# Half-empty weight block of an FFN filled with the low parts, and three reorderings, in a one-core transformer kernel

## The reference

```
base_up, base_gate = xt @ w_up.T, xt @ w_gate.T            # 704 hidden features
for e in range(8):                                          # LoRA experts, rank 16
    c = sum(where(sf == e, wf, 0))                          # weight of expert e, top 2 of 8
    h_e = silu(base_up + lo_up[e]) * (base_gate + lo_gate[e])
    ch = c * h_e
    mixed_h += ch
    lora_down += 2 * (ch @ down_A[e].T @ down_B[e].T)
out = mixed_h @ w_down.T + lora_down
```

## Time and profile before

| | |
|---|---|
| median of 3 runs | 557.07 us (556.97 to 557.43) |
| profiled execution | 557.08 us, its span 555.3 us |
| PE (matmul) | 523.4 us busy, 94% of the span |
| DVE / ACT / POOL | 402.6 (73%) / 310.6 (56%) / 126.9 (23%) |
| mean granted TensorE clock | 0.996 of full speed |
| DMA | 14.25 MB, mean 26 GB/s |

### The profile page before, as it was taken

The page is one execution under the profiler, slowest core; times in us unless marked ns, Lnnn a source line. Parts: engine busy times, 40 slices in busy tenths (PEclk is TensorE's granted clock), DMA queues, the critical chain, the costliest instruction groups (busy, mean ns, idle before and its releaser), DMA issues. The chain is left out here.

```text
span 555.3 us, 9124 instructions
## 1 busy us (share of the span) xinstructions
PE 523.4 (94%) x3049; PEld 441.6 (80%) x3049; DVE 402.6 (73%) x897; ACT 310.6 (56%) x768; POOL 126.9 (23%) x272
## 2 busy tenths in 40 slices
PE   5998899999999979999989999999998999999996
PEld 4777799999998967688878888757777778878885
DVE  5534465665665878799787899866886677878767
ACT  3655877688687643474343455988662254333332
POOL 2332434344243310000000003569433000000000
PEclk9999999999999999999999999999999999999999
DMA  7320000000002103000030000000000000000101
GB/s 267 112 78 1 18 22 2 1 1 2 2 2 102 47 1 138 1 1 1 5 129 0 2 0 1 1 1 2 1 0 2 0 1 1 1 1 0 39 1 38
DMA packets 5790, 14.25 MB, mean 26 GB/s; under 512 B 624, under 2 KB 2928, under 8 KB 5744
## 3 DMA queue, kind: packets, MB, share of 16 engines
q1 hardware_dynamic: 5744, 13.66, 6.9%
HBM read 12.61 MB, written 1.05 MB: 25 GB/s over the span
## 5 line engine op out<-in xcount | busy, mean ns | idle before, releaser
L167 PE MATMUL psum<-xT_hl,ffn_w_hl 128*128 128x512 f32 x312 | 77.8, 397 | 3.1 <-DVE f_t L1232 3.1
L167 PE MATMUL psum<-f_um,ffn_w_hl 128*128 128x512 f32 x288 | 72.6, 399 | 1.4 <-DVE f_t L1232 1.3
L167 PEld LDWEIGHTS psum<-xT_hl,ffn_w_hl 128*128 128x128 f32 x312 | 56.3, 188 | 15.0 <-issue 4.0
L167 PEld LDWEIGHTS psum<-f_um,ffn_w_hl 128*128 128x128 f32 x288 | 53.2, 188 | 14.8 <-DVE f_um L1244 3.1
L1129 ACT ACTIVATE f_sil<-psum 128x512 f32<-128x512 f32 (+1 forms) x48 | 28.6, 596 | 63.1 <-PE psum L167 62.8
L1232 DVE TENSOR_TENSOR f_t<-psum,f_sil 128x512 f32<-128x512 f32 (+1 forms) x48 | 33.2, 691 | 30.0 <-ACT f_sil L1129 29.3
L691 DVE TENSOR_TENSOR pT_hl<-psum,pT_hl 126x360 fp32r<-126x360 f32 (+1 forms) x44 | 23.6, 537 | 42.9 <-ACT pT_hl L598 42.9
L167 PE MATMUL psum<-wo_hl,oT_hl 128*128 128x256 f32 x384 | 50.8, 282 | 4.0 <-DVE oT_hl L697 4.0
L167 PE MATMUL psum<-xT_hl,wq_hl 128*128 128x512 f32 x192 | 52.3, 407 | 1.9 <-ACT qT L566 1.9
L167 PEld LDWEIGHTS psum<-wo_hl,oT_hl 128*128 128x128 f32 x384 | 47.7, 188 | 7.5 <-DVE oT_hl L697 5.9
L566 ACT ACTIVATE qT<-psum 128x512 f32<-128x512 f32 x32 | 34.9, 1091 | 31.6 <-PE psum L167 31.6
(11 more groups left out here) (238 smaller groups left out, 1130.4 us busy)
## 6 DMA issues: line engine op xcount, KB each, us to landing
w_raw<-in_wq SPq DMA_DIRECT2D x4, 512.0 KB, 4.1
w_raw<-in_wo SPq DMA_DIRECT2D x4, 512.0 KB, 3.2
ffn_w_raw<-in_ffn SPq DMA_DIRECT2D x3, 576.0 KB, 5.7
...
```

The lines of the kernel that those rows point to most:

```text
L167: i = e.matmul(dst, lhs(a), rhs(b), start=start and n == 0, stop=stop and n == len(TERMS) - 1, **kw)
```

## The change

**FFN block 5.** The down weights of block 5 are stored twice, in rows 0 to 63 and in 64 to 127 (`twice`); once, in the first FFN at ACT step 4, ACT copies the low parts of rows 0 to 63 over the high parts of these rows (`s_fwx`). The first 64 partitions of `tt` are set to zero by POOL (4 memsets a FFN), so ch and mix are zero there. ACT copies rows 64 to 127 of ch (two slots) and of mix to rows 0 to 63 of the low part, DVE writes the low part of rows 64 to 127 as before. The products of block 5 in `down` are then two matmuls with the same weight tile instead of three.

**Block 6.** `base_lora(6)` stands ahead of `second(5)` on PE. On DVE `masked` part 3 of half 1 moves ahead of `gated(4, 1)`, and parts 4 to 7 ahead of `gated(6, 0)`.

**Attention.** `oT_lo` stands ahead of `add` in each DVE step, `norm0` directly behind it, ahead of `add`; `exps` of units 0, 1, 2 lie behind the v copy of their step, unit 0 in two parts, and `recip` of units 0 and 1 one step later; query projection 7 goes to bank 7 and doesn't wait for the evacuation of projection 6.

Besides, several one-time semaphores of the router are merged in two (`top_dve`, `top_pe`); the instructions and their order are the same, and these lines are left out here.

```diff
@@ -315,7 +315,9 @@

 LAG_T, LAG_P, LAG_O, LAG_F, LAG_Y = 2, 3, 4, 5, 6
 FIRST_UNITS = {NJ - 6: 0, NJ - 4: 1, NJ - 2: 2}
-RECIPS = {NJ - 5: 0, NJ - 3: 1}
+RECIPS = {NJ - 4: 0, NJ - 2: 1}
+EXPS = {NJ - 6: (0, (0, 1)), NJ - 5: (0, (2, 3)), NJ - 4: (1, range(NB_Q)), NJ - 2: (2, range(NB_Q))}
+Q_PAIR = 2 * GROUP - 1
 NF = len(FIRST_UNITS)
 q_chunk = {NF - 1 + i: [GROUP + i] for i in range(3)}
...
@@ -439,10 +441,10 @@
         g, h = n // (2 * GROUP), n % GROUP
         half = n // GROUP % 2
         e.wait_ge(s_wl, WQ[g])
-        if n:
+        if n and n != Q_PAIR:
             e.wait_ge(s_qt, n)
         for k in range(KB):
-            m = three(e, bank(6), lambda w: wq_hl[:, g % 2, w, k, h * HD:(h + 1) * HD],
+            m = three(e, bank(7 if n == Q_PAIR else 6), lambda w: wq_hl[:, g % 2, w, k, h * HD:(h + 1) * HD],
                       lambda w: xT[:, w, k, HALF * half:HALF * half + HALF], k == 0, k == KB - 1)
         m.then_inc(s_q, 1)
...
         e.wait_ge(s_wl, WO[g])
+        e.wait_ge(s_qt, Q_PAIR + 1)
         if n:
             e.wait_ge(s_add, n)
...
-        e.activation(qT[:, HALF * half:HALF * half + HALF, h], bank(6), ACT.Copy,
+        e.activation(qT[:, HALF * half:HALF * half + HALF, h], bank(7 if n == Q_PAIR else 6), ACT.Copy,
...
-    def exps(u):
...
-        for n in range(parts):
+        for n in range(parts) if some is None else some:
             m = e.activation(p[:, n, :], p[:, n, :], ACT.Exp, bias=NEGM[0:rows, u % 4, n:n + 1],
                              accum_out=DEN[0:rows, u % 4, n:n + 1])
-        m.then_inc(s_exp, 1)
+        if n == parts - 1:
+            m.then_inc(s_exp, 1)

...
     for j in range(NJ):
-        if j in FIRST_UNITS:
-            exps(FIRST_UNITS[j])
         e.wait_ge(s_v, j + 1)
         e.activation(v_hl[0:NK[j], HI, j, :], bank(4 + j % 2)[0:NK[j], :], ACT.Copy).then_inc(s_vhi, 1)
         if j < GROUP:
             q_evac(j)
+        if j in EXPS:
+            exps(*EXPS[j])
     e.wait_ge(s_par, 16)
     e.wait_ge(s_cf, 16)
     e.activation(gw_hl[:, GW_PARTS:], cf[:, 0:GW_PAD - GW_PARTS], ACT.Copy, scale=0.0)
@@ -710,14 +714,15 @@
             recip(i - 1)
         if 0 <= i - LAG_P < NU:
             pT_lo(i - LAG_P)
+        if 0 <= i - LAG_F < NU:
+            oT_lo(i - LAG_F)
+        if i == NU + 1:
+            early(phase, "norm0", e)
         if i in y_tile:
             add(y_tile[i])
             if y_tile[i] >= (KV - 1) * NT:
                 early(phase, "stats", e, y_tile[i] % NT)
-        if 0 <= i - LAG_F < NU:
-            oT_lo(i - LAG_F)
-        for step, stage in ((NU, "veps0"), (NU + 1, "norm0"), (NU + 2, "lo0"), (NU + 3, "logits_copy0"),
-                            (NU + 4, "split0")):
+        for step, stage in ((NU, "veps0"), (NU + 2, "lo0"), (NU + 3, "logits_copy0"), (NU + 4, "split0")):
             if i == step:
                 early(phase, stage, e)

...
             da=4, dd0=4, dd=4, dh=4, dl=4, y=4, add=4)
+F_EVENTS |= dict(z=4, cx=4, mx=2)
...
@@ -1036,14 +1044,29 @@
             need(e, "dd0", 2)
         for s in range(SLOTS):
             need(e, "chl", 2 * i + s + 1)
-            m = three(e, bank(6 + s), lambda w: blk(w, b, FB_DA, ER),
-                      lambda w: ch_hl[:, i % 2, s, w, :], b == 0, b == HB - 1)
             if b == HB - 1:
+                if s == 0:
+                    e.wait_ge(s_fwx, 1)
+                need(e, "cx", 2 * h + s + 1)
+                for w in (HI, LO):
+                    m = e.matmul(bank(6 + s), blk(HI, b, FB_DA, ER), ch_hl[:, i % 2, s, w, :],
+                                 start=False, stop=w == LO)
                 m.then_inc(FS["da"], 1)
+                continue
+            three(e, bank(6 + s), lambda w: blk(w, b, FB_DA, ER),
+                  lambda w: ch_hl[:, i % 2, s, w, :], b == 0, False)
         if h == 1 and b == 0:
             need(e, "add", 2)
         need(e, "mxl", i + 1)
+        if b == HB - 1:
+            need(e, "mx", h + 1)
         for t in range(HT):
+            if b == HB - 1:
+                for w in (HI, LO):
+                    m = e.matmul(bank(4 + t // 2)[:, (t % 2) * D:(t % 2 + 1) * D],
+                                 mix_hl[:, i % 2, w, t * P:(t + 1) * P], blk(HI, b, FB_DN, D),
+                                 start=False, stop=False, skip_group_check=True)
+                continue
             m = three(e, bank(4 + t // 2)[:, (t % 2) * D:(t % 2 + 1) * D],
                       lambda w: mix_hl[:, i % 2, w, t * P:(t + 1) * P],
                       lambda w: blk(w, b, FB_DN, D),
@@ -1068,12 +1091,10 @@
                 weigh(1)
             if i == MASK_STEP + 1:
                 masks(e, 1, 0)
-            if i == MASK_STEP + 2:
-                second(i - 1)
             base_lora(e, i)
         if i == N:
             early(phase, "tr0", e)
-        if 2 <= i <= N and i != MASK_STEP + 2:
+        if 2 <= i <= N:
             second(i - 1)
         if i == MASK_STEP + 1:
             masks(e, 1, 1)
...
@@ -1145,6 +1166,9 @@
             need(e, "d", i - 1)
         need(e, f"ch{s}", i + 1)
         e.activation(ch_hl[:, i % 2, s, HI, :], ch[:, i % 2, s, :], ACT.Copy).then_inc(FS["chh"], 1)
+        if i % HB == HB - 1:
+            e.activation(ch_hl[0:REST, i % 2, s, LO, :], ch[REST:P, i % 2, s, :],
+                         ACT.Copy).then_inc(FS["cx"], 1)

     def hi_parts(i):
         if first and i == 0:
@@ -1156,6 +1180,9 @@
             weights_out(1)
         need(e, "mix", i + 1)
         e.activation(mix_hl[:, i % 2, HI, :], mix[:, i % 2, :], ACT.Copy).then_inc(FS["mxh"], 1)
+        if i % HB == HB - 1:
+            e.activation(mix_hl[0:REST, i % 2, LO, :], mix[REST:P, i % 2, :],
+                         ACT.Copy).then_inc(FS["mx"], 1)

     def lora_hi(h):
         for n, cols in enumerate(LORA_COLS):
@@ -1185,6 +1212,11 @@
             split(5)
         if i == 2:
             split(6, 7)
+        if i == MASK_STEP and first:
+            e.wait_ge(s_fwl, HB + 1)
+            stacked = slice(F_BLK + (HB - 1) * FB + FB_DN, F_BLK + HB * FB)
+            e.activation(w_hl[0:REST, HI, stacked], f32(w_hl[0:REST, LO, stacked]),
+                         ACT.Copy).then_inc(s_fwx, 1)
         if i == N - 5:
             early(phase, "w_hi0", e)
...
@@ -1285,6 +1317,8 @@
             need(e, "wbc", 2 * h + 2)
         if i >= 2:
             need(e, "chl", 2 * (i - 1))
+        if i % HB == HB - 1:
+            need(e, "z", 2 * h + s + 1)
         e.tensor_tensor(ch[:, i % 2, s, :], tt[:, s, :], wb[:, s, half(h)], ALU.mult).then_inc(FS[f"ch{s}"], 1)

...
@@ -1296,16 +1330,18 @@

     def lo_slot(i, s):
         need(e, "chh", 2 * i + s + 1)
-        e.tensor_tensor(ch_hl[:, i % 2, s, LO, :], ch[:, i % 2, s, :], f32(ch_hl[:, i % 2, s, HI, :]),
-                        ALU.subtract).then_inc(FS["chl"], 1)
+        rows = slice(REST, P) if i % HB == HB - 1 else slice(0, P)
+        e.tensor_tensor(ch_hl[rows, i % 2, s, LO, :], ch[rows, i % 2, s, :],
+                        f32(ch_hl[rows, i % 2, s, HI, :]), ALU.subtract).then_inc(FS["chl"], 1)

     def lo_parts(i):
         if i < N - 1:
             lo_slot(i, 0)
         lo_slot(i, 1)
         need(e, "mxh", i + 1)
-        e.tensor_tensor(mix_hl[:, i % 2, LO, :], mix[:, i % 2, :], f32(mix_hl[:, i % 2, HI, :]),
-                        ALU.subtract).then_inc(FS["mxl"], 1)
+        rows = slice(REST, P) if i % HB == HB - 1 else slice(0, P)
+        e.tensor_tensor(mix_hl[rows, i % 2, LO, :], mix[rows, i % 2, :],
+                        f32(mix_hl[rows, i % 2, HI, :]), ALU.subtract).then_inc(FS["mxl"], 1)

     def lora_mask(h):
         if h:
@@ -1338,12 +1374,12 @@
             a_lo(1)
         if i == MASK_STEP + 1:
             masked(1, 0, 1)
+        if i == MASK_STEP + 2:
+            masked(1, 4, 5, 6, 7)
         if i < N and i != 1:
             slot(i, 0)
         if i == MASK_STEP + 1:
-            masked(1, 2)
-        if i == MASK_STEP + 2:
-            masked(1, 4, 5)
+            masked(1, 2, 3)
         if i == HB + 3:
             early(phase, "stats", e, *range(HT))
             early(phase, "veps0", e)
@@ -1363,10 +1399,7 @@
                 slot(1, 0)
             lo_parts(i - 1)
         if i == MASK_STEP + 1:
-            masked(1, 3)
             mask_diff(1)
-        if i == MASK_STEP + 2:
-            masked(1, 6, 7)
         if 1 <= i <= 4:
             split(i + 3)
         if i == MASK_STEP - 2:
@@ -1386,7 +1419,12 @@

 def pool(e):
     ln["rstd"](e, 1)
-    early(phase, "rstd0", e)
+    for h in range(2):
+        for s in range(SLOTS):
+            need(e, f"ch{s}", HB * (h + 1) - 1)
+            e.memset(tt[0:REST, s, :], 0.0).then_inc(FS["z"], 1)
+        if h == 0:
+            early(phase, "rstd0", e)

...
 up, gate = kmaj(padh(a["ffn_w_up"], 0)), kmaj(padh(a["ffn_w_gate"], 0))
 up[..., HID:], gate[..., HID - REST:] = gate[..., HID - REST:HID], 0.0
 per_block = zip(blocks(up, P), blocks(gate, P),
```

(31 more changed lines are left out.)

21 lines of the change are left out of this document (7 added, 14 removed).

## The result

| | before | changed |
|---|---|---|
| median | 557.02 us (556.63 to 557.43, 4 runs) | 548.85 us (547.33 to 550.53, 4 runs) |
| ratio | | 0.9854, 95% interval 0.9815 to 0.9892 |
| profiled execution, its span | 557.08, 555.3 us | 550.22, 548.4 us |
| mean granted clock of it | 0.996 | 0.989 |

Faster by 1.5%. The prediction was 549.9, so it is 1.0 too high against the median and 0.3 too low against the profiled execution.

The account below looks back on a forecast made before the run. PE, busy 94% of the span with 31.9 us idle, was taken as the bound, with DVE nearly as busy at the FFN's turn of halves. The terms sum to -7.2, so 557.07 becomes 549.9 us; range 547.6 to 553.4.

Parts of the forecast that it names:

- v loop: Attention's v loop: with exponentials behind ACT's v copies, PE's waits at v tiles 7 and 9 go; -1.5 us (bounds -1.5 and 0).
- query 7: Attention: query projection 7 in bank 7 starts at once, without its 1.26 us wait for evacuation 6; -1.3 us (bounds -1.3, -0.3).
- oT_lo first, between groups: Attention: three projections no longer wait a third of a microsecond for an oT_lo behind an add; -1.0 us (bounds -1.0, 0).
- attention's end: Last 28 us of attention: oT_lo and norm0 ahead of add shorten DVE's chain; -1.7 us (bounds -3.6 and -0.3).
- block 6's order, twice: Both FFNs: base_x(7)'s 1.36 us wait goes and second(6) gains 0.28; -1.64 x 2 = -3.3 us (bounds -3.3, -1.0).
- block 5 in halves 0: First half of each FFN: 0.95 us less matmul time becomes a PE wait for DVE's add before down(6); 0 (bound -0.95 each).
- first tail: End of the first FFN: two ACT copies delay the mixer's z weights, carried on by busy DVE; +1.1 us (bounds 0, 1.8).
- second tail: End of the second FFN: one ACT copy delays mix's high part and all of lora_mask; +0.5 us (bounds 0, 1.8).
- Both thin margins: FFN block 6: gated(5, 1) done 0.3 us before PE finishes down(4), gated(4, 1) 0.2 before base_x(6); without them gain -1.0.
- Rival (b): FFN block 5: removed matmuls count in both halves 0 (-1.9) and copies in the tails cost nothing; 546.4 us, chance 0.08.
- Rival (c): Granted clock: the earlier kernel loses the 1.7 us drop at the mixer's end or gets a second; 548.2 or 551.6, chance 0.05.
- Rival (d): FFN tails: three copies between partition halves on the path are dear, 3.5 us each giving 558.8 us, slower; chance 0.03.

## Why the prediction was right

| term | predicted | changed kernel | alone |
|---|---|---|---|
| v loop | -1.5 | -1.9 | -1.74 |
| query 7 | -1.3 | -1.5 | -1.52 |
| oT_lo first, between groups | -1.0 | -0.8 | -0.67 |
| attention's end | -1.7 | -2.0 | -2.05 |
| block 6's order, twice | -3.3 | -3.9 | -3.8 |
| block 5 in halves 0 | 0 | 0 | +0.3, +0.2 with the old order |
| first tail | +1.1 | +1.6 | +1.55 |
| second tail | +0.5 | +0.7 | +0.7 |
| sum | -7.2 | -7.8 | |
| start, clock | 0 | -0.3, +1.2 | |

**Attention.** The v loop, query 7 and the end are of the size and at the place that the steps named. Between groups the size came out (0.8 for 1.0) and the place did not. The step that failed is "its users are 3 us away": the next user of the add is the very projection that waited for oT_lo, so the exchange gives nothing there. What came back is a wait that the trace of before does not show, at the bank that oT_lo frees. The near agreement of the size is chance. The waits for oT_lo that are left, 2.6 us, are also more than the 1 to 2 that I expected.

**Why the gains came out larger, 10.1 for 8.8.** I took gains from idle time shown in front of a matmul. base_x(6) to base_x(7) start to start is 9.89 us before and 8.37 after, 1.52 less, where 1.36 idle was shown. PE's ends are modelled: the last matmul ahead of a wait is drawn into the wait and hides its first 0.15 to 0.2 us. The v loop (two waits), query 7 and the order at block 6 are each short by about that much per wait.

**Block 6's order.** The 1.36 is gone in both FFNs, also in the kernel that has nothing else. Both thin margins (0.2 and 0.3 us of DVE's) held; gated(5, 1) ends 0.45 us ahead of its user, where I said 0.3, and gated(4, 1) 0.32, where I said 0.2.

**Block 5 in halves 0.** Right, by its own reason: PE comes earlier and waits for DVE. Beside the kernel without block 5's part, and counted from the f_t wait, PE is 0.91 us ahead at base_x(8) in the first FFN, 0.15 at lora_down(0), and not at all at down(6)'s second part; in the second FFN it is 0.93, 0.78 and 0.06. So the 0.9 that I put at one place is split, differently in the two. PE's busy time is 516.7 us with block 5's part and 519.2 without it, both at full clock, and 24 of its 3049 matmuls are gone; nothing of it is in the span. Rival (b), that they count, gave 546.4 and is out. One thing more than I said: with the old order at block 6 this part costs 0.3 and 0.2 us in the halves themselves, by way of masked 7.

**The tails.** The mechanism was right and the size off. First tail: the copies take 0.63 each, not 0.60; the z weights come later by the two I counted, 1.2 of the 1.6, and 0.4 comes from the memset that meets xn. Second tail: 0.7 for 0.5, one copy of 0.63 and its handover. I had put POOL's memsets at nothing, "since few of them meet DVE on the path"; one did. Their own price was low too: 0.52 instead of the 0.45 that I scaled from the earlier trace rows.
The Trainium skill (GPSIMD Engine Reference, Specifications) names as contention DVE instructions in a 2-port mode or with two SBUF inputs. The traces agree for a CAST on POOL beside a sum of two SBUF tiles (0.69 to 1.13). They don't for a memset beside that sum, which leaves both as they are (0.52 and 0.69), while the instructions that the memset did slow, xn's, have a single tile as input. Whether xn runs in a 2-port mode no row shows. Of the price that I worked out from that rule, up to 3.6, the 0.4 at xn is what was found, and not at f_ch, where I had put it.

**The clock.** Rival (c) was that a shift by some us loses a drop or gets a second one, at 551.6. The profiled execution has the second one, in the last tail; it costs 2.90 - 1.64 = 1.26 us, and the trace stands at 550.22, below 551.6 since the orders gave more than forecast. Of nine runs of the changed kernel three had clock 1.00 (547.3 to 547.5), the others 0.989 to 0.997 (549.4 to 550.6). With block 6's new order and without block 5's part 11 of 13 runs had 1.00. So the median of the changed kernel depends on how many of its runs have a drop, and the 548.85 and 550.16 of its two medians are the same thing with another share.

Drops were seen at the end of the mixer (0.57 to 0.63 over 4 us), in the last tail (0.50 to 0.57) and once in the first FFN's tail. What they have in common in the rows is that PE was partly idle in the 4 us ahead: busy for 2.97 of 4.00 at 416, 2.48 at 536. But the execution with clock 1.00 has the same 2.97 at 416, and in its last tail 2.47 over 534.5 to 538.5 and 1.91 over 536 to 540, without a drop. So idle time comes before every drop and doesn't make one each time; what decides stays open. That block 5's part makes drops likelier (longer waits in both tails) is not shown. The counts of 3 in 9 against 11 in 13 look like it, but the kernel before, which has no such part, had clock 1.00 in only 4 of 33 runs, and with block 5's part alone it was 2 of 4; no run took the waits away with the copies left in.

**Rival (d)** needed 2.9 us a copy; they took 0.63.

The forecast of the sum was thus right with errors that cancel: gains 1.3 too small, tails 0.7 too cheap, a drop of the clock for 1.2 not counted. That it fits to 1 us is in part luck. Of the range, the low end was added up wrongly: the parts that it names, 0.95 and 1.9 below 549.9, make 547.0 and not 547.6; the result lies above both.
